# One delta*u buffer and newly dealt slots in a fused Mamba-and-experts layer, and another order at the end of the last expert

## The reference

```python
u, res = split(x @ W_in)                      # 512 inner channels
u = silu(conv3(u)); dt, B, C = split(u @ W_x) # rank 16, 16 states
delta = softplus(dt @ W_dt + b_dt)
h = exp(delta * A) * h + (delta * u) * B      # for each of 16 states, along 1024 tokens
y = (sum over states of h * C + u * D) * silu(res)
x = layernorm(x + y @ W_out)
# experts: top 2 of 8, capacity 1280 tokens an expert
out = layernorm(x + sum of share * ((silu(x @ wg) * (x @ wu)) @ wd))
```

## Time and profile before

| | |
|---|---|
| median of three runs | 2394.84 us (2394.42 to 2395.79) |
| the profiled execution | 2394.69 us |
| its span | 2392.8 us |
| PE / DVE / POOL / ACT busy | 94% / 90% / 77% / 73% |

### The profile page before, as it was taken

One profiled execution on the slowest core, in us unless ns is written; L12 is line 12 of the kernel. 1 busy time (PEld: TensorE's weight loads), 2 busy tenths in 40 slices (PEclk: granted clock), 3 DMA queues, 4 the chain that ended last, 5 costly groups with the idle time before them and its releaser, 6 DMA issues. The chain is left out here.

```text
span 2392.8 us, 39513 instructions
## 1 busy us (share of the span) xinstructions
PE 2245.3 (94%) x14183; PEld 1809.9 (76%) x14183; DVE 2145.2 (90%) x2917; ACT 1746.1 (73%) x2935; POOL 1851.2 (77%) x1028
## 2 busy tenths in 40 slices
PE   9999999999999999999999997745999999999995
PEld 5677777777777777777777766634999999999995
DVE  6999999999999999999999999986787787787775
ACT  6989989999899999998998998842344344434355
POOL 5899999999999999999999999952336437436465
PEclk9999999999999999999999999966999999999998
DMA  3222222222122222221222211122122322322353
GB/s 114 63 62 72 72 80 71 72 71 81 62 72 72 80 71 72 71 81 62 72 72 80 72 63 62 62 71 75 32 67 45 87 65 45 88 64 44 89 200 135
DMA packets 88722, 178.93 MB, mean 75 GB/s; under 512 B 9152, under 2 KB 51904, under 8 KB 88528
## 3 DMA queue, kind: packets, MB, share of 16 engines
q1 hardware_dynamic: 73648, 154.11, 19.4%
q0 software_dynamic: 14880, 22.29, 5.2%
HBM read 140.20 MB, written 36.18 MB: 74 GB/s over the span
## 5 line engine op out<-in xcount | busy, mean ns | idle before, releaser
L1105 DVE TENSOR_TENSOR_SCAN hst<-da,dbu 128x512 f32<-128x512 f32 x1008 | 1173.4, 1209 | 15.5 <-ACT da L806 10.1
L612 POOL TENSOR_TENSOR dbu<-du,b_all 128x2048 f32<-128x2048 f32 x254 | 1154.5, 4546 | 22.3 <-DVE hst L1105 22.3
L806 ACT ACTIVATE da<-delta,a_neg 128x512 f32<-128x512 f32 x1008 | 695.3, 699 | 101.4 <-DVE hst L1105 96.1
L2447 PE MATMUL gu<-x_part,w_part 128*128 128x384 f32 (+1 forms) x2304 | 485.8, 360 | 3.1 <-DVE x_part L2194 1.7
L2447 PEld LDWEIGHTS gu<-x_part,w_part 128*128 128x128 f32 x2304 | 402.9, 189 | 34.1 <-issue 4.5
L1272 PEld LDWEIGHTS hd<-ident,hst 128*128 128x128 f32 x2040 | 240.3, 141 | 187.3 <-issue 121.2
L772 ACT ACTIVATE hTC<-w,c_tok 128x512 f32<-128x512 f32 x510 | 350.1, 687 | 18.1 <-PE w L1272 12.8
L1190 PE MATMUL gen<-xT,w_u 128*128 128x512 f32 x720 | 360.9, 597 | 0.1
L1272 PEld LDWEIGHTS w<-ident,hst 128*128 128x128 f32 x2040 | 243.2, 141 | 142.9 <-issue 97.3
L1272 PE MATMUL hd<-ident,hst 128*128 128x128 f32 x2040 | 312.9, 276 | 35.9 <-DVE yacc L991 27.3
L991 DVE SCALAR_TENSOR_TENSOR yacc<-hd,c_tok,yacc 128x512 f32<-128x512 f32 x457 | 335.0, 733 | 12.6 <-PE hd L1272 7.6
(11 more groups left out here) (348 smaller groups left out, 2829.3 us busy)
## 6 DMA issues: line engine op xcount, KB each, us to landing
b_all<-b_rows SPq DMA_DIRECT2D x128, 512.0 KB, 3.7
xT<-in_xT SPq DMA_DIRECT2D x16, 514.0 KB, 5.0
xT_r<-in_xT SPq DMA_DIRECT2D x16, 512.0 KB, 5.0
x_rows<-in_x SPq DMA_DIRECT2D x16, 512.0 KB, 3.8
w_raw<-in_wg SPq DMA_DIRECT2D x8, 1024.0 KB, 5.0
w_raw<-in_wu SPq DMA_DIRECT2D x8, 1024.0 KB, 8.3
w_raw<-in_wd SPq DMA_DIRECT2D x8, 1024.0 KB, 10.7
x_dram<-x SPq DMA_DIRECT2D x15, 512.0 KB, 3.0
```

The source lines that it names most:

```text
L612: nc.gpsimd.tensor_tensor(dbu[DBU[n]][:], du[parity][:], b_n, ALU.mult).then_inc(dbu_ready, 1)
L806: nc.scalar.activation(da_bank[t % 2][:], delta[parity][:, t, :], ACT.Exp, scale=a_neg[:, t, n:n + 1]).then_inc(da_ready, 1)
L1105: nc.vector.tensor_tensor_scan(hst[DBU[n]][:, t, :], decay[:], dbu[DBU[n]][:, t, :], 0.0, ALU.mult, ALU.add).then_inc(scanned, 1)
L2447: last = nc.tensor.matmul(gu_bank[n % 2][i][:, 0:width(n)], gu_part[wp][:, i, kk, f * P:(f + 1) * P], x_part[xp][:, kk, tokens_of(j)], sta ...
```

## The change

- `du` has one buffer. POOL multiplies it at the end of a chunk, behind `dbu` of state 15. That `dbu` is made in four instructions of 128x512, each waiting only for the scan of its own tile of state 13.
- The freed buffer (`held`) takes stashes: one moves there from `yT`, and chunk 14 has a third one. The scratch of the expert choice moves to `w_r` and `xT_r`, the staging of `W_in` to `dbu[2]`.
- Nearly all slot tables have new numbers.
- In the last expert five tiles are measured in each of the first four steps, and four after that; ACT normalises group `i` in step `i + 8`; of the last two groups ACT takes two tiles and POOL two; the first own tiles are normalised in step 23, behind the last group.

```diff
@@ slots (the core of the tables)
-    "r0": (0, 0, 0), "r1": (1, 0, 6), "C0": (0, 2), "r2": (0, 4, 5), "C1": (0, 6, 8, 9, 10, 12),
-    "r3": (1, 8, 10), "o0": (0, 15, 15, 16, 18), "o1": (1, 21, 22, 23, 23), "xd": (0, 21, 23, 24, 24),
+    "r0": (0, 0, 0), "r1": (1, 0, 5), "C0": (0, 2), "r2": (0, 4, 4), "C1": (0, 7, 8, 10, 10, 13),
+    "r3": (1, 12, 12), "o0": (0, 15, 16, 18, 19), "o1": (1, 21, 22, 23, 23), "xd": (0, 21, 23, 24, 24),
...
-    "u1": (1, 36, 39, 39, 40, 41, 43), "d3": (0, 38), "u2": (1, 45, 47, 47, 47, 48, 49), "ud0": (0, 45),
-    "xt0": (0, 48), "xt1": (0, 53), "u3": (1, 54, 55, 56, 57, 60, 61), "ud1": (0, 54), "lg": (0, 56, 57, 60, 62),
+    "u1": (1, 36, 39, 39, 41, 41, 43), "d3": (0, 38), "u2": (1, 45, 45, 47, 47, 48, 50), "ud0": (0, 45),
+    "xt0": (0, 49), "xt1": (0, 52), "u3": (1, 54, 55, 57, 57, 58, 61), "ud1": (0, 54), "lg": (0, 58, 59, 60, 61),
...
-    "r0": 2, "r1": 8, "C0": 3, "C1": 12, "r2": 6, "r3": 12, "xd": 26, ...
+    "r0": 2, "r1": 9, "C0": 3, "C1": 12, "r2": 6, "r3": 14, "xd": 26, ...
-SUM_LATE_AT = 25
+SUM_LATE_AT = 24
-ACC_READ_AT = (7, 12)
+ACC_READ_AT = (8, 9)
-EXP_AT = (42, 47)
-LN_AT = (49, 50)
-NORM_AT = (39, 43, 45, 49)
+EXP_AT = (42, 45)
+LN_AT = (48, 50)
+NORM_AT = (40, 43, 44, 49)
-SMALL_AT = 11
+SMALL_AT = 8
-DU_AT = 15
-STASH = {c: {5: "extra", 6: "gap", 14: "row0"} for c in range(TOK // CL)}
-STASH[CHUNKS - 2] = {5: "w0", 6: "w1"}
+STASH = {c: {5: "extra", 6: "v0", 14: "row0"} for c in range(TOK // CL)}
+STASH[CHUNKS - 2] = {5: "w0", 6: "w1", 14: "w2"}
@@ chunk 0
-    "v0": (0, 0, 0, 0, 1, 1, 2), "v1": (1, 0, 0, 2, 2, 3, 3), "v2": (0, 2, 2, 3, 3, 3, 3),
-    "v3": (1, 4, 4, 5, 5, 8, 10), "r0": (0, 7, 8), "r1": (0, 10, 12), "r2": (1, 14, 14), "r3": (0, 15, 16),
-    "xd": (0, 19, 20, 22, 24), ...
+    "v0": (0, 0, 0, 0, 0, 0, 2), "v1": (1, 0, 0, 0, 2, 2, 2), "v2": (0, 2, 2, 3, 3, 3, 3),
+    "v3": (1, 3, 3, 4, 5, 6, 8), "r0": (0, 6, 6), "r1": (0, 11, 11), "r2": (1, 14, 14), "r3": (0, 15, 18),
+    "xd": (0, 20, 21, 21, 26), ...
@@ POOL, chunk
-                        nc.gpsimd.tensor_tensor(du[other][:], delta[other][:], u[:], ALU.mult).then_inc(du_ready, 1)
...
+                        if n == NST - 1:
+                            for t in range(DT):
+                                pool.wait_ge(scanned, c * SLOTS + DT * done + t + 1)
+                                ins = nc.gpsimd.tensor_tensor(dbu[DBU[n]][:, t, :], du[:, t, :], b_n[:, 0, :], ALU.mult)
+                            ins.then_inc(dbu_ready, 1)
...
+                if s.front:
+                    if s.main:
+                        pool.wait_ge(dbu_ready, (c + 1) * NST)
+                    pool.wait_ge(u_ready, c + 2)
+                    nc.gpsimd.tensor_tensor(du[:], delta[other][:], u[:], ALU.mult).then_inc(du_ready, 1)
@@ last expert
-ON_ACT = [3] * NG
-FIRST_NORM_AT, NORM_LAG = 5, 4
-MEASURE_OWN_AT = {15: 0, 22: 1}
-OWN_NORM_AT = 21
+ON_ACT = [3] * (NG - 2) + [2, 2]
+FIRST_NORM_AT, WIDE_STEPS, NORM_LAG = 5, 4, 3
+MEASURE_OWN_AT = {15: 0, 21: 1}
+OWN_NORM_AT = 23
...
-                if k == 6:
+                if k == 7:
                     add_own(1)
...
+            def norm_step(n):
+                first, last = tiles_until(n), tiles_until(n + 1)
+                for m in range(first, last):
+                    if m == first + 2:
+                        for i in range(first // G):
+                            aggregate(i)
+                    measure(m // G, m % G)
+                if first == last:
+                    aggregate(NG - 1)
+            def tiles_until(n):
+                return min(NG * G, n * G + min(n, WIDE_STEPS))
```

More of the change, by code:

```diff
@@ L143 @@
 FIRST_EXP_AT = (43, 46)
-FIRST_LN_AT = (48, 50)
+FIRST_LN_AT = (49, 51)
 class Stage:
@@ L273, in attention @@
         delta = [sb(f"delta{i}", [P, DT, CL]) for i in range(2)]
-        du = [sb(f"du{i}", [P, DT, CL]) for i in range(2)]
+        du = sb("du", [P, DT, CL])
+        held = sb("held", [P, DT, CL])
         xdT = sb("xdT", [P, CL])
@@ L304, in attention @@
                       for i in range(N_TAPS * KD)})
+        stash.update({f"v{i}": held[:, i, :].rearrange("p (t q) -> p t q", q=P) for i in range(DT)})
         stash.update({f"x{i}": xT[:, i, 0:CL].rearrange("p (t q) -> p t q", q=P) for i in range(KD)})
@@ L389, in attention @@
         tops = {}
-        for buffer, names in ((delta[0], TOP_WIDE[:4]), (du[0], TOP_WIDE[4:])):
+        for buffer, names in ((delta[0], TOP_WIDE[:4]), (w_r, TOP_WIDE[4:6]), (xT_r, TOP_WIDE[6:])):
             flat = buffer[:].rearrange("p t c -> p (t c)")
@@ L412, in attention @@
         b_rows = dram["b_rows"]
-        w_staging = du[1][:].rearrange("p a b -> p (a b)")[:, 0:KD * DI].rearrange("p (k d) -> p k d", k=KD)
+        w_staging = dbu[2][:].rearrange("p a b -> p (a b)")[:, 0:KD * DI].rearrange("p (k d) -> p k d", k=KD)
         HALF_PADDED = (SEQ + 2) // 2
@@ L566, in chunk @@
                                                 ).then_inc(delta_ready, 1)
-                    if n == DU_AT and s.front:
+                    if n == NST - 1 and s.front:
                         pool.wait_ge(delta_ready, c + 1)
@@ L582, in chunk @@
                         done = n - DBU_BACK[n]
+                        b_n = b_all[n // BG % 2][:, n % BG:n % BG + 1, :]
+                        if n == NST - 1:
[3 more added lines that the diff above has]
+                            ins.then_inc(dbu_ready, 1)
+                        elif done >= 0 or s.close:
+                            pool.wait_ge(scanned, c * 64 + 4 * done + 4)
                         if done >= 0 or s.close:
-                            pool.wait_ge(scanned, c * 64 + 4 * done + 4)
                             if done >= 0 and parity == 0 or n == 0 and parity == 1:
@@ L606, in chunk @@
                             for t in range(DT):
-                                ins = nc.gpsimd.tensor_tensor(dbu[DBU[1]][:, t, :], du[0][:, t, :], b_all[0][:, 1, :],
+                                ins = nc.gpsimd.tensor_tensor(dbu[DBU[1]][:, t, :], du[:, t, :], b_all[0][:, 1, :],
                                                               ALU.mult)
@@ L610, in chunk @@
                             continue
-                        b_n = b_all[n // BG % 2][:, n % BG:n % BG + 1, :].to_broadcast([P, DT, CL])
-                        nc.gpsimd.tensor_tensor(dbu[DBU[n]][:], du[parity][:], b_n, ALU.mult).then_inc(dbu_ready, 1)
+                        if n < NST - 1:
+                            nc.gpsimd.tensor_tensor(dbu[DBU[n]][:], du[:], b_n.to_broadcast([P, DT, CL]), ALU.mult
+                                                    ).then_inc(dbu_ready, 1)
                         if parity == 1:
@@ L782, in stash_state @@
                     act.wait_ge(u_ready, CHUNKS)
-                elif s.c == CHUNKS - 1:
+                elif s.c == CHUNKS - 1 or buffer[0] == "v" and s.close:
                     act.wait_ge(ring_full, s.nth_full("C1") + 1)
@@ L969, in lead_terms @@
                 dve.wait_ge(lead_du if not last else du_ready, t + 1 if not last else 1)
-                nc.vector.tensor_tensor(dbu[DBU[0]][:, t, :], du[0][:, t, :], b_all[0][:, 0, :], ALU.mult
+                nc.vector.tensor_tensor(dbu[DBU[0]][:, t, :], du[:, t, :], b_all[0][:, 0, :], ALU.mult
                                         ).then_inc(lead_dbu if not last else dbu_ready, 1)
@@ L2209, in measure, with aggregate @@
                     if i >= 2:
+                        aggregate(i - 2)
                         dve.wait_ge(aggregated, (i - 1) * G)
                 v.bn_stats(stats[i % 2][:, g, :], rows[i % ROW_BUFFERS][:, g, :]).then_inc(measured, 1)
-            def norm_step(i):
-                if i < NG:
-                    measure(i, 0)
-                    measure(i, 1)
-                if i > 0:
-                    dve.wait_ge(measured, i * G)
-                    for g in range(G):
-                        v.bn_aggr(mean_var[i - 1][:, g, :], stats[(i - 1) % 2][:, g, :]).then_inc(aggregated, 1)
-                if i < NG:
-                    measure(i, 2)
-                    measure(i, 3)
+            def aggregate(i):
+                if i < groups_done[0]:
+                    return
+                groups_done[0] = i + 1
+                dve.wait_ge(measured, (i + 1) * G)
+                for g in range(G):
+                    v.bn_aggr(mean_var[i][:, g, :], stats[i % 2][:, g, :]).then_inc(aggregated, 1)
+            groups_done = [0]
+            def norm_step(n):
[9 more added lines that the diff above has]
+                return min(NG * G, n * G + min(n, WIDE_STEPS))
             def measure_own(j):
@@ L2288, in expert @@
                             own_index()
[L2289 removed]
+                        if 0 <= n - FIRST_NORM_AT <= NG - WIDE_STEPS // G:
                             norm_step(n - FIRST_NORM_AT)
```

21 lines of the change are left out of this document (10 added, 11 removed), and 8 rows, old and new, of tables (FILL_AT, FIRST_FILL_AT).

## The result

The kernel after takes 2404.03 us (median of 6 runs, 2403.87 to 2404.90) against 2394.29 us: ratio 1.0041, 95% interval 1.0031 to 1.0052. It is slower by 9.7 us; the forecast was 2395.3 us, "the same", with 2387.5 to 2399.5 us, and "slower" had 0.16. The waits forecast for the last expert came out within about 0.2 us; the first part of the kernel did not.

The account below looks back on a forecast made before the run. The prediction took DVE as busiest, with PE and POOL close behind, and POOL's chain as setting even chunk ends. It summed +3.3 - 2.8 - 1.6 + 1.6 = +0.5 us to 2395.3 us, range 2387.5 to 2399.5.

Parts of the forecast that it names:

- part 2: New slot tables in the chunks: -0.2 us in chunks 1 to 14, -2.8 us; 0 for slots 48 to 51.
- Part 1: Chunk ends, `du` behind `dbu` 15 in four pieces: +0.41 us at each of 8 even ends, +3.3 us; odd ends nothing.
- rival on the slots: Slots of the chunks: the new tables remove DVE's idle time, about -9 us, 2386 us; chance 0.17.
- first rival: `dbu` 8 in each chunk: POOL's moved small work makes DVE's scan wait, +10.5 us, 2405.8 us; chance 0.12.
- rival on the tail: Last expert: ACT finds group 2 ready or PE is not held; sum -4.7 us, 2390.6 us; chance 0.13.
- Part 3: Chunk 0: first `xd` part moves behind the turn, DVE's 2.12 us of idle time at 68.83 goes; -1.6 us together.
- Part 4: Last expert: ACT stands 3.1 us before group 2, PE's gap grows to 3.9 us at lost clock; +1.6 us.

Follow-up runs that it names:

- e10: Kernel before with only ACT's second exponential moved from slot 47 to 45 and its `u1` read to 45; 2405.62 us, ratio 1.0045.
- e9: Kernel after with only ACT's second exponential back at slot 47 and its `u1` read at 46; 2396.1 us, ratio 1.0007.
- e7: Kernel after with two `du` buffers and old order, ACT's old slots 38 to 52, and `gather_own(2)` moved to k == 4; 2386.99 us, ratio 0.9971.
- e8: Kernel after, one `du` buffer kept, with ACT's old slots 38 to 52 and `gather_own(2)` moved to k == 4; 2392.36 us, ratio 0.9994.
- e1: Kernel before with only the single `du` buffer and the new order at the chunk's end; old slots and tail; ratio 1.0010.
- e12: e7 with slots 38 to 52 as in the kernel after, except the second exponential and its `u1` read; 2386.63 us, ratio 0.9969.
- e2: Kernel after with two `du` buffers and the old order at the chunk's end; new slots and tail kept; ratio 1.0023.
- e3: Kernel after with only ACT's slots 38 to 52 (with the `u2` and `xt0` fills) as before; ratio 1.0014.
- e4: Kernel after with POOL's small work back in front of state 11 instead of state 8; ratio 1.0039.
- e5: Kernel before with only the last expert's new tail; ratio 1.0009.
- e6: Kernel after with `gather_own(2)` of the last expert moved from k == 1 to k == 4, so POOL serves `root(1)` first; 2401.57 us, ratio 1.0028.
- e11: e7 with group 2 of the last expert normalised one step later, behind the eviction PE waits for; 2389.11 us, ratio 0.9975.

## Why the prediction was wrong

**The step that failed** is in part 2: "The bigger waits lie in slots 48 to 51 ... It only lies in other slots of the stretch ... So I book 0". It took ACT's work over ten slots as one sum. What decides is the order: two numbers, the exponential from slot 47 to 45 and its `u1` read, cost +10.7 us on the kernel before (e10) and 8 us in the kernel after (e9 against after). The same sentence had the reason in it: ACT's lead is under 1 us, and with a read and an exponential ahead of one `da` (in e10 a normalisation too) the scan that needs it stood 0.60 us in after and 0.72 in e10. And the idle time of slots 48 to 51, 0.7 us a chunk rather than the 1.0 of the prediction, was only in part ACT's: in before 0.27 us of it ends with `da`, and 0.30 with PE's `hd`, which stands behind three `u2` parts. The earlier trace rows named PE's `hd` as what ended 3.9 us of the additions' waits, and the step passed over it. The prediction itself said that slots 48 to 51 should still have a gap; in after they have none above 0.1 us.

**Why it counts in full.** The prediction knew that POOL's chain runs from state 11 to the next chunk's first scan, and used it in one direction only: "what DVE gains after slot 47 of an even chunk is given back". The other side is that what DVE loses before slot 47 starts the chain later and is not hidden, while idle time behind slot 47 lies beside the chain as long as it is shorter than the chain. Cut at the end of scan 47, the chunks show it (us, read from the starts and ends of the scans):

| kernel | first scan to the end of scan 47 | from there to the next first scan, even / odd | idle behind scan 47, to slot 52 |
|---|---|---|---|
| before | 71.28 | 24.59 / 24.12 | 0.71 |
| after | 71.70 | 25.03 / 24.02 | 0.08 |
| e9 | 71.00 | 25.07 / 24.02 | 0.54 |
| e7 | 71.00 | 24.54 / 24.09 | 0.67 |
| e10 | 72.08 | 24.45 / 24.34 | 1.12 |

After and e9 differ by 0.70 us ahead of the cut and by nothing behind it, though after has nearly no idle time left there. The new tables moved idle time from behind slot 47, where it cost little, to before it, where it is paid in every chunk. In e10, with 1.12 us of it, the odd chunks pay for a part behind the cut as well.

**Part 1, +3.3.** Right in kind, too small in size: 0.56 us an even end rather than 0.41, all eight ends in e8 against e7 (+4.5 us), and 0 at odd ends, as forecast (e1). The four pieces take the forecast 0.4 us more than one. But that 0 rested on 0.7 us of slack at the odd end, which e12 shows was not the chain's, and with the stall before slot 46 the odd periods of after are 0.31 longer than before, while the same stall without the order makes them 0.39 longer (e2).

**Part 2, the rest.** Slot 11's -0.2 us came (no wait there in after, e3 or e7), and with the right slots around it a chunk is 0.31 to 0.33 us shorter (e7). The rival on the slots was right that the three `u2` parts cost idle time, but dealing them as in the change gained nothing in e12. POOL's small work costs nothing: the scan of slot 32 starts without a wait, POOL stands 3.38 us before it (predicted 3.6), and e4 finds no difference. The first rival did not occur. The rival on the tail has a slip in its sum, 2390.6 for 2394.8 - 4.7 = 2390.1, which changes nothing.

**Part 3, -1.6.** The profile of after has chunk 0 at 106.23 us against 107.75. Part 1's order is in this number too. With two buffers the old tables gave 107.75 and 107.76 (before, e10) but 106.35 in e5; the new ones 105.63 to 105.68 (four profiles). With one buffer the old ones gave 106.92 (e1), the new ones 106.17 to 106.23 (six). In before and e10 the granted clock is 0.50 from 66 to 70 us, as in the earlier trace rows, in e5 and e1 it stays at 1.00, and the idle time at 68.83, on which this part rests, is then 0.84 us instead of 2.12:

```profile
67.45 0.75 DVE L991 SCALAR_TENSOR_TENSOR yacc<-hd,c_tok,yacc 128x512 f32<-128x512 f32 x1 [0.84 <-PE hd L1272]
68.00:69.00 1.00, 1.00 (x8) 0.74 (x8) 0.25 (x2) 0.99 (x2) 1.00 (x1) 1.00 0.00 0
```

(both of e5). So at equal order and clock the tables gain 0.7 us in chunk 0, and the order takes 0.56 of it back; the rest of the -1.5 us measured is a fall of the clock that the profile of before had here and that of after did not. The -1.6 was close by luck.

**Part 4, +1.6.** The place, the 3.1 us and the 3.9 us were right, and the fall of the clock too. The total was +1.2 in the traces compared and up to +3.6 with a longer slow stretch. The trace of after agrees with the rule quoted from the Trainium skill ("TensorE: Matmul & The Clock Gate", Part 1: The HAM clock gate): behind the idle stretch of 3.91 us the clock is 0.50, and back at 1.00 after a busy one.

With the failed step taken from e9 (+8 for 0), the sum is +8.5 against +9.7 measured; the rest is within what the single terms vary by. Why the clock falls in chunk 0 or 1 in some profiles and not in others is open. That DVE's late aggregate is all that keeps 1.8 us of PE's gap in e6 was read from the trace, not tried.

## What to carry to other kernels

When two engines pass work to each other once a period, find where the chain that sets the period starts: idle time beside it is free as long as it fits beside the chain, and the same idle time ahead of it is paid in full, in every period. So book a moved instruction by the two instructions it now stands between and by the wait of who needs the later one, never by the sum over a stretch. Where a chain was found to swallow gains on one side, ask at once what it does with losses on the other.

## What the runs showed of the hardware

The same pause of PE does not always cost the clock. In the last expert of e6, e7, e8 and e12 a pause of 1.80 to 1.82 us stands before the same down product. In e6 and e7 a granted clock of 0.50 (1.2 of 2.4 GHz) for some 3 us followed, in e8 and e12 it stayed at 1.00. PE's product and the clock about a microsecond behind it, in e7 and in e8:

```profile
2319.79 1.59 PE L2479 MATMUL dn<-w_part,hid_part 128*128 128x256 f32 x9 [1.80 <-ACT eo L2358]
2321.00:2322.00 1.00, 1.00 (x5) 1.00 (x5) 1.00 (x5) 0.90 (x2) 1.00 (x2) 0.50 0.84 328
2324.05 1.31 PE L2493 MATMUL dn<-w_part,hid_part 128*128 128x256 f32 x9 [1.82 <-ACT eo L2372]
2325.00:2326.00 1.00, 1.00 (x9) 1.00 (x8) 1.00 (x4) 1.00 (x3) 1.00 (x2) 1.00 0.70 283
```

From the last scan to the end it is 831.7 and 831.9 us in e6 and e7, 830.0 and 829.0 in e8 and e12. So a single profile can't tell a gain of 2 us in this place from whether the clock happened to fall, and e11's profile, with a pause of 2.59 us, a clock of 1.00 throughout and 829.5 us, is one more such case. A pause of 3.9 us was followed by 3.4 us at half clock in one profile (after) and went with 6.8 us in two (e5, e9). Pauses of 1.26 us before the last down products cost no clock before PE's work was done. Chunks 0 and 1 show the same twice over (e4 and part 3 above), and it can enter a forecast unseen: a wait read where PE was at half clock, 2.12 us, was 0.84 at full clock.

One program also differs by 27 us between two chips (medians of the kernel before, 2394.3 and 2421.5 us). It was not profiled on the second, but e1 to e4 were: their first parts are as elsewhere, and in their experts PE stood 12 to 13 us in all for "issue", time in which it waited for nothing that the profile shows, between 1700 and 2300 us, which it never did in the other profiles. That is about half of the difference; the other half is open.
